# One store for the transposed logit rows, and W1's columns in blocks of 32, in a two-layer graph kernel

## The chip, the cores and the metric

One core of a Trainium2 chip. The metric is the device time of one execution in microseconds, median of the runs. The batch holds 128 graphs of 128 nodes with 512 features.

## The reference, cut to what matters

Each graph goes through a graph-attention layer and then a two-step hypergraph layer, each with a layer norm in front and a residual around it.

```python
# layer 0, per graph: h = relu(layernorm(x))
feats = einsum('bnf,hfu->bhnu', h, W)                   # 8 heads x 64
dense = e_self[..., :, None] + e_neigh[..., None, :]    # needs e_neigh of all nodes in every row
att   = softmax(leaky_relu(dense, 0.2) + NEG_BIG * (1 - A))
x     = x + relu(einsum('bhij,bhju->bhiu', att, feats) + b)
# layer 1: h = relu(layernorm(x)); H = (adj != 0)
r = relu(Dn * (H @ (Be * (H.T @ (h @ W1.T)))) + b1)     # 128 x 1024
h = layernorm(r) * gamma + beta
x = x + Dn * (H @ (Be * (H.T @ (h @ W2.T)))) + b2 + x
```

## The kernel before, in words

One graph is one turn; the instruction stream of each engine is written out by hand in a function `turn(t)`, and `turns` calls it for the first turns, for a loop unrolled by four, and for the last. A turn works on several graphs at once: it does attention's end for graph t+1, the projections of graph t+3, W1's product for graph t and W2's product for graph t-1. Products are made of three matmuls each (`three`, `high`, `low`), since every operand is split into a rounded half (`_hi`) and a remainder (`_lo`). In a turn TensorE does, in this order: W1's product into `p_w1a` and `p_w1b` (lines 866 and 869), the last product of graph t-2 into `p_tb` (898), the attention transposes (907), half of the projections (919), the attention product (927), W2's product (941 and 944), `p_w1b` from `h` and `G_rs` (957), the rest of the projections, and `p_G` (976).

Two things cross the partitions through DRAM, both on the queue of SyncE (SP), and both are touched by the change.

- **Logit rows.** `e_blk` holds 32 columns for each of the 128 nodes: the neighbour logits of the 8 heads and, for a later graph, the mean of its layer norm (9 rows wanted, `ROWS`). VectorE's transpose by blocks of 32 (line 651) gives `eT`, in which the 32 rows stand four times, once for each block of 32 nodes. Lines 275 and 276 store them with four DMAs of 9 partitions x 32 elements into `en_rows`, one semaphore (`s_en_out`) counts all four, line 277 waits for it, and line 278 reads `en_rows` back, broadcast to all 128 partitions, into `u`. GpSimd adds the mask to `u` (line 338) and then makes `xc` (347). VectorE takes the maximum (731) and, in order behind it, `shifts` (740), the attention's division and `x1` (747 to 757), the statistics of `x1` (760 to 778), `G_rs` (783) and `z` (797); ScalarE makes `h` (538), `z_hi` (547) and `hg_hi` (554). TensorE needs `h` and `G_rs` at line 957 and `hg_hi` at the start of the next turn.
- **r's transpose.** `r` is 128 x 1024. VectorE transposes it by blocks of 32 (line 722) into `rB`; line 289 stores it, line 290 waits, and lines 291 to 293 read it back with four DMAs. Each reads, for one quarter of a block row, runs of 32 elements (128 bytes): 32 partitions x 8 x 4 runs, 1,024 in a DMA. ScalarE rounds `rT` to `rT_hi` (561), VectorE takes the rest, `rT_lo` (658), and TensorE uses both a turn later (941, 944).

The four lines of the logit rows:

```python
for q in range(4):
    sp.dma_start(en_rows[:, 32 * q:32 * (q + 1)], eT[32 * q:32 * q + ROWS, :]).then_inc(s_en_out, 16)
sp.wait_ge(s_en_out, g.count(per=64))
sp.dma_start(u[:, g.slot(2), :, :]..., en_rows...broadcast_to([P, ROWS * N])).then_inc(s_en_bc, 16)
```

SP's order in a turn is: load `xT` of t+4, load `adj` of t+5, the logit rows, the store of the output of t-2, the store of `r_blocks` and its four reads. `x` is loaded by ScalarE's queue.

Of the kernel before, what the change touches and what calls it, by code (L numbers as in the profile page):

```python
# [4 lines left out]
F32 = mybir.dt.float32  # L5
F32R = mybir.dt.float32r
ALU = mybir.AluOpType
ACT = mybir.ActivationFunctionType
X = mybir.AxisListType.X

P = 128
# [38 lines left out]
def turns(eng, turn, total, before={}):  # L50


    loops = (total - AHEAD - 3) // UNROLL
    for t in range(-AHEAD, 2):
        if t in before:
            before[t]()
        turn(Graph(t))
    with eng.Fori(0, loops) as k:
        for u in range(2, UNROLL + 2):
            turn(Graph(u, k))  # L60
    for t in range(2 + loops * UNROLL, total + 2):
        turn(Graph(t))


def gnn_two_layers(nc, x, xT, adj2, W0T, W0U, b0, a_diag, W1T, b1, gammaT, betaT, W2T, b2, out):
    NG, N, D = x.shape
# [11 lines left out]
    ROWS = HEADS + 1  # L78

    ctx = ExitStack()  # L80
    with ctx:
        def sb(name, shape, dt=F32):
            return ctx.enter_context(nc.sbuf_tensor(name, shape, dt))

        def sem(name):
            return ctx.enter_context(nc.semaphore(name))
# [43 lines left out]
        eT = sb("eT", [P, 32])  # L130
# [10 lines left out]
        h = sb("h", [P, 2, D])  # L141
# [2 lines left out]
        r = raw[:, 2, 0:DH]  # L144
        rB = raw[:, 0, 0:DH]
        rT = raw[:, 0, DH:2 * DH]
        rT_hi, rT_lo = sb("rT_hi", [P, DH], F32R), sb("rT_lo", [P, DH], F32R)
        z = raw[:, 1, 3 * D:4 * D]
        z_hi, z_lo = sb("z_hi", [P, D], F32R), sb("z_lo", [P, D], F32R)
# [31 lines left out]
        s_e_blk, s_es_low, s_eT, s_en_out, s_en_bc, s_u = (sem("s_" + n) for n in ("e_blk", "es_low", "eT", "en_out", "en_bc", "u"))  # L181
# [7 lines left out]
        s_nm2a, s_nm2, s_sq2, s_ve2, s_rs2, s_rB, s_rB_out, s_rT, s_rT_hi, s_rT_lo = (sem("s_" + n) for n in ("nm2a", "nm2", "sq2", "ve2", "rs2", "rB", "rB_out", "rT", "rT_hi", "rT_lo"))  # L189
        s_w2, s_z, s_z_hi, s_z_lo, s_y, s_y_sb = (sem("s_" + n) for n in ("w2", "z", "z_hi", "z_lo", "y", "y_sb"))  # L190
        s_G_hi, s_G_lo = sem("s_G_hi"), sem("s_G_lo")

        en_rows = nc.dram_tensor("en_rows", [ROWS, N], F32, kind="Internal").ap()

        r_blocks = nc.dram_tensor("r_blocks", [P, DH], F32, kind="Internal").ap()

# [13 lines left out]
        def piece(n):  # L210
            return raw[:, n % 4, :].rearrange("p (c n) -> p c n", c=4)
# [12 lines left out]
        @block.sync  # L224
        def _(sp):
            def nth(g):
                return g.base if g.loop is None else g.loop * UNROLL + g.base

            def load_x(g):

                sp.dma_start(x_in[:, g.slot(4), :], x[bass.ds(nth(g), 1), :, :].rearrange("a p d -> p (a d)")).then_inc(s_in[g.slot(4)], 16)

            def load_adj(g):

                if g.has(4):
                    sp.wait_ge(s_inc, g.count(4))
                    sp.wait_ge(s_mask, g.count(4))
                    sp.wait_ge(s_row, g.count(4))
                sp.dma_start(adj_in[:, g.slot(4), :, :], adj2[bass.ds(nth(g), 1), :, :, :].rearrange("a p t n -> p (a t) n")).then_inc(s_in[g.slot(4)], 16)

            def load(g):
                load_x(g)
                load_adj(g)

            def load_xT(g):

                if g.has(2):
                    sp.wait_ge(s_xc, g.count(2))
                sp.dma_start(xT_in[:, g.slot(2), :, :],
                             xT[bass.ds(nth(g), 1), :, :, :].rearrange("a p c n -> p (a c) n")).then_inc(s_xT[g.slot(2)], 16)  # L250

            def load_last_piece():

                sp.wait_ge(k_hi, 1)
                sp.wait_ge(k_lo0, 1)
                sp.dma_start(piece(4), PIECES[4][0]).then_inc(s_raw[4], 16)

            def bc(v, n):
                return v.rearrange("(a n) -> a n", a=1).broadcast_to([P, n])

            load(Graph(0))
            load_xT(Graph(0))
            sp.dma_start(a_sb[:, :, :, :], a_diag).then_inc(s_vectors, 16)
            load(Graph(1))

            def turn(t):
                g = t.plus(4)
                if g.within(NG) and (g.loop is not None or g.base >= 2):
                    load_xT(g)
                if t.plus(5).within(NG) and (t.loop is not None or t.base >= -1):  # L270
                    load_adj(t.plus(5))
                if g.within(NG + 2):

                    sp.wait_ge(s_eT, g.count())
                    for q in range(4):
                        sp.dma_start(en_rows[:, 32 * q:32 * (q + 1)], eT[32 * q:32 * q + ROWS, :]).then_inc(s_en_out, 16)
                    sp.wait_ge(s_en_out, g.count(per=64))
                    sp.dma_start(u[:, g.slot(2), :, :].rearrange("p h n -> p (h n)"),
                                 en_rows.rearrange("(a h) n -> a (h n)", a=1).broadcast_to([P, ROWS * N])).then_inc(s_en_bc, 16)
                g = t.plus(-2)  # L280
                if g.within(NG):

                    sp.wait_ge(s_y_sb, g.count())
                    sp.dma_start(out[bass.ds(nth(g), 1), :, :].rearrange("a p d -> p (a d)"), y[:, g.slot(2), :]).then_inc(s_out[g.slot(2)], 16)
                g = t
                if g.within(NG):

                    sp.wait_ge(s_rB, g.count())
                    sp.dma_start(r_blocks[:, :], rB).then_inc(s_rB_out, 16)
                    sp.wait_ge(s_rB_out, g.count(per=16))  # L290
                    for c in range(4):
                        sp.dma_start(rT[32 * c:32 * (c + 1), :].rearrange("a (k q b) -> a k q b", q=4, b=32),
                                     r_blocks.rearrange("(q a) (k c b) -> c a k q b", q=4, c=4, b=32)[c]).then_inc(s_rT, 16)

            def setup_rest():
                load_xT(Graph(1))
                sp.dma_start(b0_bc[:, :], bc(b0.rearrange("h u -> (h u)"), D)).then_inc(s_small, 16)
                sp.dma_start(gamma_beta[:, 0, :], gammaT).then_inc(s_small, 16)
                sp.dma_start(gamma_beta[:, 1, :], betaT).then_inc(s_small, 16)
                load(Graph(2))  # L300
                load(Graph(3))
                sp.dma_start(b1_bc[:, :], bc(b1, DH)).then_inc(s_small, 16)
                sp.dma_start(b2_bc[:, :], bc(b2, D)).then_inc(s_small, 16)
                load_last_piece()

            turns(sp, turn, NG, {-3: setup_rest})
            for i in range(2):
                sp.wait_ge(s_out[i], 16 * (NG // 2))
# [96 lines left out]
        def _(act):  # L405
# [37 lines left out]
            def turn(t):  # L443
# [3 lines left out]
                g = t.plus(3)  # L447
# [6 lines left out]
                g = t  # L454
# [4 lines left out]
                g = t  # L459
# [5 lines left out]
                g = t.plus(2)  # L465
# [7 lines left out]
                g = t  # L473
# [3 lines left out]
                g = t.plus(1)  # L477
# [11 lines left out]
                g = t  # L489
# [13 lines left out]
                g = t.plus(-1)  # L503
# [5 lines left out]
                g = t  # L509
# [5 lines left out]
                g = t  # L515
# [8 lines left out]
                g = t.plus(5)  # L524
                if g.within(NG) and (g.loop is not None or g.base >= 4):

                    act.wait_ge(s_x1, g.count(4))
                    n = g.base if g.loop is None else g.loop * UNROLL + g.base
                    act.dma_start(x_in[:, g.slot(4), :], x[bass.ds(n, 1), :, :].rearrange("a p d -> p (a d)")).then_inc(s_in[g.slot(4)], 16)
                g = t.plus(1)  # L530
# [10 lines left out]
                g = t.plus(-1)  # L541
# [6 lines left out]
                g = t.plus(1)  # L548
# [6 lines left out]
                g = t  # L555
                if g.within(NG):

                    act.wait_ge(s_rT, g.count(per=64))
                    if g.has(1):
                        act.wait_ge(s_w2, g.count(1))  # L560
                    nc.scalar.activation(rT_hi[:, :], rT, ACT.Copy).then_inc(s_rT_hi, 1)  # L561
                g = t.plus(2)
                if g.within(NG):

# [11 lines left out]
            def setup_w2b():  # L576
                rounded(4)

            turns(act, turn, NG, {-2: setup_w1a, -1: setup_w1b, 0: setup_w2b})

        @block.vector
        def _(dve):
# [35 lines left out]
            def turn(t):  # L618
                g = t.plus(2)
# [34 lines left out]
                g = t.plus(-1)  # L654
                if g.within(NG):

                    dve.wait_ge(s_rT_hi, g.count())
                    nc.vector.tensor_tensor(rT_lo[:, :], rT, rT_hi[:, :], ALU.subtract).then_inc(s_rT_lo, 1)
                g = t
                if g.within(NG):  # L660

# [8 lines left out]
                g = t.plus(3)  # L670
# [5 lines left out]
                g = t.plus(2)  # L676
# [8 lines left out]
                g = t.plus(2)  # L685
# [13 lines left out]
                g = t  # L699
# [4 lines left out]
                g = t.plus(-2)  # L704
# [8 lines left out]
                g = t  # L713
# [13 lines left out]
                g = t.plus(2)  # L727
# [14 lines left out]
                g = t.plus(1)  # L742
# [18 lines left out]
                g = t.plus(2)  # L761
# [8 lines left out]
                if t.plus(1).within(NG):  # L770
                    g = t.plus(1)
# [18 lines left out]
                g = t.plus(-1)  # L790
# [8 lines left out]
                g = t.plus(5)  # L799
# [11 lines left out]
                if g.within(NG):  # L811
                    nc.vector.bn_aggr(mv0, st0[:, :]).then_inc(s_mv0, 1)

            turns(dve, turn, NG, {-3: setup_w0})

        @block.tensor
# [204 lines left out]
```

## Time and profile before

| | |
|---|---|
| median of 3 runs | 2489.99 us (2489.61 to 2491.07) |
| the profiled execution | 2479.36 us |
| its span, first to last instruction | 2477.6 us |
| TensorE busy | 2419.2 us, 98% of the span |
| VectorE, ScalarE, GpSimd busy | 1976.4, 1763.3, 1368.0 us |
| mean granted TensorE clock | 0.991 |
| DMA | 656,793 packets, 336.69 MB; 554,752 packets under 512 bytes |

The busy time of an engine is the sum of its instructions' time, in which overlapping matmuls count once; the ends of matmuls are modelled. An idle time stands in brackets behind an instruction in the timeline, with what ended it. SPq is SyncE's queue: a row of it is the issuing of a DMA, not its flight.

### The profile page before, as it was taken

What the parts mean: (1) busy time and instruction counts of PE and PEld (TensorE: products, weight loads), DVE (VectorE), ACT (ScalarE), POOL (GpSimd) and SP (SyncE); (2) the same over time, 40 slices, a digit from 0 to 9 for tenths busy, and PEclk for the clock granted to TensorE, in tenths of its full rate; (3) what the DMA queues carried; (4) which work ended last, traced back from release to release, by engine and by line L of the source; (5) the groups of instructions that cost most, each with busy time, mean ns of one, the idle gap of its engine ahead of it and who ended that gap; (6) DMA issues with size and microseconds to landing.
All of it is one profiled execution on the core that took longest, in us unless ns stands there. A gap on an engine that the chain in (4) does not pass through costs nothing.

```text
span 2477.6 us, 50428 instructions
## 1 busy us (share of the span) xinstructions
PE 2419.2 (98%) x14004; PEld 2101.6 (85%) x14004; DVE 1976.4 (80%) x4373; ACT 1763.3 (71%) x4489; POOL 1368.0 (55%) x1549
## 2 busy tenths in 40 slices
PE   5799999999999999999999999999999999999997
PEld 3688888888888888888888888888888888888886
DVE  3888888888888888888888888888888888888884
ACT  2677777777777777777777777777777777777774
POOL 2465555565565565565555555555555556556543
PEclk8899999999999999999999999999999999999999
DMA  5344454455445445445445445445454444445442
GB/s 206 95 139 138 136 140 137 134 140 140 134 139 141 134 139 141 134 138 142 132 138 143 131 139 143 125 145 139 128 142 137 134 138 138 137 137 138 138 113 72
DMA packets 656793, 336.69 MB, mean 136 GB/s; under 512 B 554752, under 2 KB 571136, under 8 KB 656768
## 3 DMA queue, kind: packets, MB, share of 16 engines
q1 hardware_dynamic: 636256, 298.64, 43.5%
q10 hardware_dynamic: 20512, 37.76, 4.3%
q8 instruction: 11, 0.18, 0.0%
q14 instruction: 14, 0.11, 0.0%
HBM read 235.03 MB, written 101.26 MB: 136 GB/s over the span
## 4 chain that ended last, share of the span: by engine, by line
PE 95%; DMA 2%; DVE 1%; issue 1%; ACT 1%; POOL 0%; SPq 0%; POOLq 0%; DVEq 0%; ACTq 0%
PE p_w1a L853 15%; PE p_w1a L858 14%; PE p_w1a L854 14%; PE p_att L927 9%; PE p_w1b L854 5%; PE p_w1b L858 5%; PE p_w1b L853 5%; PE p_w1b L957 5%; PE p_att L907 4%; PE p_fa L849 3%; PE p_fa L847 3%; PE p_fa L848 3%; PE p_fb L847 2%; PE p_fb L848 2%; PE p_fb L849 2%; PE p_tb L847 1%
## 5 line engine op out<-in xcount | busy, mean ns | idle before, releaser
L338 POOL TENSOR_TENSOR u<-u,mask 128x1024 f32<-128x1024 f32 x128 | 306.6, 2395 | 761.4 <-DMA u<-en_rows 761.4
L438 ACT ACTIVATE att<-u,shifts 128x128 f32<-128x128 f32 x1024 | 402.3, 393 | 133.0 <-DVE shifts L740 131.6
L853 PE MATMUL p_w1a<-W_hi,rT_hi 128*128 128x512 f32 x1024 | 416.8, 407 | 1.5 <-ACT rT_hi L561 1.5
L854 PE MATMUL p_w1a<-W_lo,rT_hi 128*128 128x512 f32 x1024 | 405.9, 396 | 0.0
L439 ACT ACTIVATE att_low<-u,shifts 128x128 f32<-128x128 f32 x1024 | 399.6, 390 | 0.0
L731 DVE TENSOR_REDUCE neg_max<-u 128x8 f32<-128x1024 f32 x128 | 156.1, 1220 | 149.9 <-POOL u L338 149.9
L858 PE MATMUL p_w1a<-W_hi,rT_lo 128*128 128x512 f32 x1024 | 259.5, 395 | 0.0
L392 POOL TENSOR_TENSOR z_lo<-raw,z_hi 128x512 fp32r<-128x512 f32 x128 | 165.7, 1294 | 154.9 <-ACT z_hi L547 154.9
L927 PE MATMUL p_att<-feats,attT 128*128 128x65 f32 x2048 | 243.1, 272 | 3.1 <-ACT attT L483 3.1
L927 PEld LDWEIGHTS p_att<-feats,attT 128*128 128x128 f32 x2048 | 239.5, 192 | 3.9 <-ACT attT L483 3.9
L547 ACT ACTIVATE z_hi<-raw 128x512 fp32r<-128x512 f32 x128 | 81.1, 634 | 221.6 <-DVE raw L797 221.6
L858 PEld LDWEIGHTS p_w1a<-W_hi,rT_lo 128*128 128x128 f32 x1024 | 192.4, 188 | 46.6
L853 PEld LDWEIGHTS p_w1a<-W_hi,rT_hi 128*128 128x128 f32 x1024 | 194.0, 189 | 42.5 <-ACT rT_hi L561 2.0
L854 PEld LDWEIGHTS p_w1a<-W_lo,rT_hi 128*128 128x128 f32 x1024 | 193.7, 189 | 40.6
L476 ACT ACTIVATE raw<-raw 128x512 f32<-128x512 f32 x128 | 80.8, 631 | 192.1 <-DVE raw L702 192.1
L853 PE MATMUL p_w1a<-W_hi,hg_hi 128*128 128x512 f32 x512 | 213.9, 418 | 2.2 <-ACT hg_hi L554 2.2
L853 PE MATMUL p_w1b<-W_hi,hg_hi 128*128 128x512 f32 x512 | 202.7, 396 | 0.0
L854 PE MATMUL p_w1b<-W_lo,hg_hi 128*128 128x512 f32 x512 | 202.3, 395 | 0.0
L854 PE MATMUL p_w1a<-W_lo,hg_hi 128*128 128x512 f32 x512 | 202.1, 395 | 0.0
L362 POOL TENSOR_TENSOR raw<-x,raw 128x512 f32<-128x512 f32 x128 | 166.1, 1298 | 26.9 <-DVE shifts L740 26.9
L347 POOL TENSOR_TENSOR xc<-xT_in,u 128x512 f32<-128x512 f32 x128 | 167.4, 1308 | 22.4 <-DMA u<-en_rows 22.4
L610 DVE TENSOR_TENSOR att<-att,att_low 128x512 f32<-128x512 f32 x256 | 174.3, 681 | 4.8 <-ACT att_low L439 4.8
(121 smaller groups left out, 6759.7 us busy)
## 6 DMA issues: line engine op xcount, KB each, us to landing
u<-en_rows SPq DMA_DIRECT2D x130, 576.0 KB, 3.6
r_blocks<-raw SPq DMA_DIRECT2D x128, 512.0 KB, 2.6
raw<-r_blocks SPq DMA_DIRECT2D x512, 128.0 KB, 3.2
xT_in<-in_xT SPq DMA_DIRECT2D x128, 256.0 KB, 3.9
out<-raw SPq DMA_DIRECT2D x128, 256.0 KB, 2.0
x_in<-in_x ACTq DMA_DIRECT2D x124, 256.0 KB, 3.6
adj_in<-in_adj SPq DMA_DIRECT2D x128, 128.0 KB, 2.5
en_rows<-eT SPq DMA_DIRECT2D x520, 1.1 KB
```

What stands on the lines that cost most here:

```text
L338: nc.gpsimd.tensor_tensor(u[:, g.slot(2), 0:HEADS, :], u[:, g.slot(2), 0:HEADS, :], mask[:, :].unsqueeze(1).broadcast_to([P, HEADS, N]), A ...
L347: nc.gpsimd.tensor_tensor(xc[:, :, :], xT_in[:, g.slot(2), :, :], u[:, g.slot(2), HEADS, :].unsqueeze(1).broadcast_to([P, DC, N]), ALU.sub ...
L362: nc.gpsimd.tensor_tensor(rest[s4], x1[:, s, :], rest[s4], ALU.add).then_inc(s_xh, 1)
L392: nc.gpsimd.tensor_tensor(z_lo[:, :], z[:, :], z_hi[:, :], ALU.subtract).then_inc(s_z_lo, 1)
L438: nc.scalar.activation(att[:, i, :], u[:, g.slot(2), i, :], ACT.Exp, bias=shifts[:, 0, i:i + 1])
L439: last = nc.scalar.activation(att_low[:, i, :], u[:, g.slot(2), i, :], ACT.Exp, bias=shifts[:, 1, i:i + 1], scale=SLOPE)
L610: nc.vector.tensor_tensor(att[:, heads, :], att[:, heads, :], att_low[:, heads, :], ALU.max).then_inc(s_att, 1)
L731: nc.vector.reduce_max(neg_max[:, :], u[:, g.slot(2), 0:HEADS, :], X, negate=True).then_inc(s_max, 1)
L853: mm(dst, hi, w_hi, start=first, stop=False)
L854: mm(dst, hi, w_lo, start=False, stop=False)
L858: return mm(dst, lo, w_hi, start=False, stop=final)
L927: last = mm(p_o[:, i // HH, i % HH, :], attT[:, i, :], feats[:, g.slot(2), i, :], start=True, stop=True)
```

## The change

The four stores of logit rows become one: all 128 partitions of `eT` are stored, 32 elements each, into an `en_rows` of 32 rows in place of 9, of which the broadcast reads the first 9 as before. The wait behind it counts 16 in place of 64. The columns of W1 and the entries of b1 are laid out on the host in another order (`by_blocks`), with which `r`'s columns that one of the four reads fetches stand next to each other: each read takes runs of 256 elements (1 KB), 32 partitions x 4 runs, 128 in a DMA. The data in `rT` then stand in another order within a partition, and lines 561 and 658 read them through a view of four dimensions (`rT_chunks`) in runs of 32 elements; what they write is laid out as before. The rest of the kernel is as it was.

```diff
--- before.py
+++ after.py
@@ -144,6 +144,7 @@
         r = raw[:, 2, 0:DH]
         rB = raw[:, 0, 0:DH]
         rT = raw[:, 0, DH:2 * DH]
+        rT_chunks = rT.rearrange("p (q k a) -> p k q a", q=4, a=32)
         rT_hi, rT_lo = sb("rT_hi", [P, DH], F32R), sb("rT_lo", [P, DH], F32R)
         z = raw[:, 1, 3 * D:4 * D]
         z_hi, z_lo = sb("z_hi", [P, D], F32R), sb("z_lo", [P, D], F32R)
@@ -190,7 +191,7 @@
         s_w2, s_z, s_z_hi, s_z_lo, s_y, s_y_sb = (sem("s_" + n) for n in ("w2", "z", "z_hi", "z_lo", "y", "y_sb"))
         s_G_hi, s_G_lo = sem("s_G_hi"), sem("s_G_lo")
 
-        en_rows = nc.dram_tensor("en_rows", [ROWS, N], F32, kind="Internal").ap()
+        en_rows = nc.dram_tensor("en_rows", [32, N], F32, kind="Internal").ap()
 
         r_blocks = nc.dram_tensor("r_blocks", [P, DH], F32, kind="Internal").ap()
 
@@ -272,11 +273,10 @@
                 if g.within(NG + 2):
 
                     sp.wait_ge(s_eT, g.count())
-                    for q in range(4):
-                        sp.dma_start(en_rows[:, 32 * q:32 * (q + 1)], eT[32 * q:32 * q + ROWS, :]).then_inc(s_en_out, 16)
-                    sp.wait_ge(s_en_out, g.count(per=64))
+                    sp.dma_start(en_rows.rearrange("h (q a) -> q h a", a=32), eT[:, :]).then_inc(s_en_out, 16)
+                    sp.wait_ge(s_en_out, g.count(per=16))
                     sp.dma_start(u[:, g.slot(2), :, :].rearrange("p h n -> p (h n)"),
-                                 en_rows.rearrange("(a h) n -> a (h n)", a=1).broadcast_to([P, ROWS * N])).then_inc(s_en_bc, 16)
+                                 en_rows[0:ROWS, :].rearrange("(a h) n -> a (h n)", a=1).broadcast_to([P, ROWS * N])).then_inc(s_en_bc, 16)
                 g = t.plus(-2)
                 if g.within(NG):
 
@@ -289,8 +289,8 @@
                     sp.dma_start(r_blocks[:, :], rB).then_inc(s_rB_out, 16)
                     sp.wait_ge(s_rB_out, g.count(per=16))
                     for c in range(4):
-                        sp.dma_start(rT[32 * c:32 * (c + 1), :].rearrange("a (k q b) -> a k q b", q=4, b=32),
-                                     r_blocks.rearrange("(q a) (k c b) -> c a k q b", q=4, c=4, b=32)[c]).then_inc(s_rT, 16)
+                        sp.dma_start(rT[32 * c:32 * (c + 1), :].rearrange("a (q n) -> a q n", q=4),
+                                     r_blocks.rearrange("(q a) (c n) -> c a q n", q=4, c=4)[c]).then_inc(s_rT, 16)
 
             def setup_rest():
                 load_xT(Graph(1))
@@ -558,7 +558,7 @@
                     act.wait_ge(s_rT, g.count(per=64))
                     if g.has(1):
                         act.wait_ge(s_w2, g.count(1))
-                    nc.scalar.activation(rT_hi[:, :], rT, ACT.Copy).then_inc(s_rT_hi, 1)
+                    nc.scalar.activation(rT_hi[:, :].rearrange("p (k q a) -> p k q a", q=4, a=32), rT_chunks, ACT.Copy).then_inc(s_rT_hi, 1)
                 g = t.plus(2)
                 if g.within(NG):
 
@@ -655,7 +655,8 @@
                 if g.within(NG):
 
                     dve.wait_ge(s_rT_hi, g.count())
-                    nc.vector.tensor_tensor(rT_lo[:, :], rT, rT_hi[:, :], ALU.subtract).then_inc(s_rT_lo, 1)
+                    nc.vector.tensor_tensor(rT_lo[:, :].rearrange("p (k q a) -> p k q a", q=4, a=32), rT_chunks,
+                                            rT_hi[:, :].rearrange("p (k q a) -> p k q a", q=4, a=32), ALU.subtract).then_inc(s_rT_lo, 1)
                 g = t
                 if g.within(NG):
 
@@ -997,6 +998,10 @@
     for k, a in enumerate((L0_gnn_a_neigh, L0_gnn_a_self)):
         for p in range(2):
             a_diag[p, :, :, k, p] = np.asarray(a)[p::2, :].T
+    def by_blocks(a):
+
+        return a.reshape(a.shape[:-1] + (-1, 4, 32)).swapaxes(-3, -2).reshape(a.shape)
+
     laid = {
         "x": x,
         "xT": np.asarray(x).transpose(0, 2, 1).reshape(len(x), -1, P, np.asarray(x).shape[1]).transpose(0, 2, 1, 3),
@@ -1004,7 +1009,7 @@
         "W0T": np.asarray(L0_gnn_W).transpose(1, 0, 2).reshape(f, -1),
         "W0U": np.asarray(L0_gnn_W).transpose(0, 2, 1).reshape(-1, f),
         "b0": L0_gnn_b, "a_diag": a_diag.reshape(2 * units, heads // 2, 2, 2),
-        "W1T": np.asarray(L1_gnn_W1).T, "b1": L1_gnn_b1,
+        "W1T": by_blocks(np.asarray(L1_gnn_W1).T), "b1": by_blocks(np.asarray(L1_gnn_b1)),
         "gammaT": np.asarray(L1_gnn_gamma).reshape(-1, P).T, "betaT": np.asarray(L1_gnn_beta).reshape(-1, P).T,
         "W2T": np.asarray(L1_gnn_W2).T, "b2": L1_gnn_b2,
     }
```

## Rows read from the trace of the kernel before

**Rows 1.** Page, part 1: busy time of each engine.

```profile
PE 2419.2 (98%) x14004; PEld 2101.6 (85%) x14004; DVE 1976.4 (80%) x4373; ACT 1763.3 (71%) x4489; POOL 1368.0 (55%) x1549
```

**Rows 2.** Busy time of each engine in one stretch of 200 us.

```profile
1000.00:1200.00 200.00, 199.99 (x1164) 174.20 (x1164) 164.35 (x368) 147.44 (x379) 114.52 (x131) 1.00 0.49 137
```

**Rows 3.** Waits of TensorE: total, times, longest, in us.

```profile
PE p_w1b L957 <- ACT h L538: 14.1, 2, 10.6
```

**Rows 4.** Timeline of TensorE, line 976 alone: start, duration; six turns of 128.

```profile
114.32 0.39 PE L976 MATMUL p_tb<-beT,inc 128*128 128x129 f32 x2
...
1679.35 0.39 PE L976 MATMUL p_tb<-beT,inc 128*128 128x129 f32 x2
...
1698.35 0.39 PE L976 MATMUL p_tb<-beT,inc 128*128 128x129 f32 x2
...
2034.65 0.39 PE L976 MATMUL p_tb<-beT,inc 128*128 128x129 f32 x2
...
2201.99 0.39 PE L976 MATMUL p_tb<-beT,inc 128*128 128x129 f32 x2
...
2407.06 0.39 PE L976 MATMUL p_tb<-beT,inc 128*128 128x129 f32 x2
```

**Rows 5.** Timeline of the turn from 1679.35, SP, GpSimd, VectorE and TensorE.

```profile
1681.53 1.37 SPq L276 DMA_DIRECT2D en_rows<-eT  x4
1683.80 0.34 SPq L278 DMA_DIRECT2D u<-en_rows  x1
...
1687.67 2.37 POOL L338 TENSOR_TENSOR u<-u,mask 128x1024 f32<-128x1024 f32 x1 [6.43 <-DMA u<-en_rows]
...
1695.72 0.31 DVE L783 TENSOR_SCALAR G_rs<-G,rs 128x128 f32<-128x128 f32 x1 [0.71 <-POOL rs L373]
...
1696.28 1.15 PE L957 MATMUL p_w1b<-G_rs,h 128*128 128x128 f32 x8
```

**Rows 6.** Timeline of the turn from 2164.80, the same two engines.

```profile
2171.94 2.41 POOL L338 TENSOR_TENSOR u<-u,mask 128x1024 f32<-128x1024 f32 x1 [5.59 <-DMA u<-en_rows]
...
2181.42 1.05 PE L957 MATMUL p_w1b<-G_rs,h 128*128 128x128 f32 x8
```

**Rows 7.** Page, part 6: DMA issues, KB each, median us to landing.

```profile
r_blocks<-raw SPq DMA_DIRECT2D x128, 512.0 KB, 2.6
...
out<-raw SPq DMA_DIRECT2D x128, 256.0 KB, 2.0
...
adj_in<-in_adj SPq DMA_DIRECT2D x128, 128.0 KB, 2.5
```

**Rows 8.** Issues of r_blocks on SP: duration ns min/median/max.

```profile
L292 SPq DMA_DIRECT2D raw<-r_blocks x512: 568/683/1488, 88.2 to 2458.5; - x171
L289 SPq DMA_DIRECT2D r_blocks<-raw x128: 319/327/385, 85.6 to 2453.8; - x128
```

**Rows 9.** Chain that ended last, first 60 us, two of four stores.

```profile
22.40 7.52 DMA en_rows<-eT
...
35.41 1.19 DMA en_rows<-eT
```

**Rows 10.** Timeline of the last turn, SP, ScalarE and TensorE.

```profile
2456.47 2.75 SPq L292 DMA_DIRECT2D raw<-r_blocks  x4
...
2461.53 1.06 ACT L561 ACTIVATE rT_hi<-raw 128x1024 fp32r<-128x1024 f32 x1 [2.79 <-DMA raw<-r_blocks]
...
2460.71 0.40 PE L849 MATMUL p_tb<-z_hi,G_lo 128*128 128x512 f32 x1
2462.64 0.80 PE L853 MATMUL p_w1a<-W_hi,rT_hi 128*128 128x512 f32 x1 [1.54 <-ACT rT_hi L561]
```

**Rows 11.** VectorE by line: busy, mean ns of one, idle before it.

```profile
L731 DVE TENSOR_REDUCE neg_max<-u 128x8 f32<-128x1024 f32 x128 | 156.1, 1220 | 149.9 <-POOL u L338 149.9
...
L749 DVE TENSOR_TENSOR p_ta<-p_att,rden 128x512 f32<-128x512 f32 x128 | 89.6, 700 | 4.4
...
L757 DVE SCALAR_TENSOR_TENSOR x<-p_ta,x_in 128x512 f32<-128x512 f32 x128 | 88.5, 691 | 4.4
```

## The prediction, made before the change was run

> **What bounds the kernel now.** The page's first part gives TensorE 98% of the time, VectorE 80% [rows 1], and a stretch of 200 us in the middle has TensorE busy all through [rows 2]. The list of its waits agrees: the large ones lie in the first 100 us and the last 65, as the one of 10.6 us for `h` [rows 3]. By these three views only the two ends could be won. But the ends of matmuls are modelled, so a late start can hide in a busy time. The fourth view therefore is the start of one fixed instruction in each turn (line 976) [rows 4]. The nine turns from 2034.65 to 2201.99 take 167.34 us, 18.593 each: TensorE's own pace. The 123 turns from 114.32 to 2407.06 take 2292.74 us; at 18.593 they would take 2286.97. So **5.8 us** are lost in the middle, in small pieces, where no wait is listed. The turn from 1679.35 to 1698.35 alone takes 19.00, which is 0.41 too long.
>
> What do the long turns have in common? In that one GpSimd's mask addition, released by the landing of `u<-en_rows`, starts 8.32 us after the turn's line 976; in a turn at the pace of 18.59 it starts 7.14 after it [rows 5, 6]. From there the chain runs through VectorE's maximum, the attention's end and `G_rs`; `G_rs` ends at 1696.03 and line 957, which needs it, starts 0.25 later, 16.93 into the turn, where the other turn has it at 16.62. So TensorE is held 0.31 us there, and the rest of the 0.41 follows at `hg_hi`, made behind it. The slack of this chain ends where the mask addition starts some 8.0 us into the turn (8.32 less 0.31). It is also nearly a loop: VectorE's `eT` stands in its order behind `hg_lo` of the turn before, so a late `u` makes the next `eT` late. I went through all 124 turns in this way: the turns over 18.63 are those with the latest `u`, or the ones just behind them. The store of the logit rows lies on this chain.
>
> **The change, part by part.**
>
> *One store for four.* From the first issue to the broadcast behind the wait there are 2.27 us (1681.53 to 1683.80), of which four issues take 1.37, 0.34 each [rows 5]. The last starts at about 1682.56, so a store of 9 packets has landed 1.2 us after its issue; the chain gives 1.19 for one in the first turns [rows 9]. Three issues go, 1.03 us. What comes in their place is a store of 128 packets of 128 bytes, which the trace does not have. From below it is the 1.2 of 9 packets. From above it is the output's store, also one packet for each of 128 partitions, but 256 KB: 2.0 us; `r_blocks`, 512 KB, takes 2.6 [rows 7], so the size costs 0.6 per 256 KB, and at 16 KB that line comes down to 1.4. Small writes may be dearer than their bytes, so I take 1.6, the middle of 1.2 and 2.0. The broadcast then starts 2.27 - 1.6 = 0.67 us earlier in each turn; the bounds are 0.27 and 1.07.
>
> In the middle this buys no TensorE time as such; it moves `u` from 8.32 to 7.65 in the latest turn, below 8.0. It would do so with 0.32 already. Term: **-5.8 us**; at the bound of 0.27 the latest turns keep a little, say -5. What is late next is TensorE itself, so nothing more is to be had: 18.593 is the floor.
>
> In the first turns there are four such stores on the chain that sets the start. Two of them land under the load of the weights and `x`, 7.52 us after the last issue in the worse case [rows 9]; their landing is not set by when they are issued, and I take nothing, with 1 us either way. The other two are as in the middle, on the chain before TensorE's continuous work begins: 2 x 0.67 = **-1.3 us** (0.5 to 2.1).
>
> *The reads of r's transpose.* Each has 1,024 packets and takes 0.683 us to issue; an issue with 128 packets, `r_blocks`' own store, takes 0.327 [rows 8]. Four reads: 1.4 us less of SP's time in each turn, in which only `xT` and `adj` stand behind them, loaded turns ahead. `rT_hi` is ready long before its use in the next turn, so in the middle the gain is worth nothing. In the last turn nothing covers it. There the reads are issued from 2456.47 on, in 2.75 us, and ScalarE starts `rT_hi` at 2461.53 [rows 10]. At 0.36 from issue to issue the last one starts at 2457.55; `adj_in` is 128 KB in runs of 1 KB as well and lands in 2.5 us [rows 7], so `rT_hi` starts at 2460.05. Term: **-1.5 us**. TensorE, which now starts at 2462.64, would start at 2461.1; its product in front has its last start at 2460.71 [rows 10], so not much more than 1.6 can come. If the landing stays as it is, 1.05. The first seven matmuls behind this wait are 0.43 us apart where 0.23 is usual, at the lower level of the clock; if the shorter wait spares that, up to 1.3 us more, which I leave to the range.
>
> *The view in runs of 32* in lines 561 and 658: the nearest row is line 749, which works in runs of 64 with a gap, 700 ns, beside line 757, contiguous, 691 ns [rows 11]. Nothing, or 0.02 us; VectorE's wait for `u`, 149.9 / 128 = 1.17 us a turn [rows 11], covers it, and still 0.5 of it is there when `u` comes 0.67 sooner. The host's order of W1 and b1 costs nothing: the same loads, the same columns to TensorE.
>
> **Sum:** 5.8 + 1.3 + 1.5 = 8.6 us. The profiled execution's 2479.36 becomes 2470.8; the median is 10.6 us longer than that execution, and with the same difference it becomes **2481.4 us**, -0.35%. About 0.2% (5 us) is what a measurement of this kernel can tell from no change.
>
> **Rivals.**
>
> *Only the ends (0.22).* The 5.8 us stay, because something else than `u` makes the long turns, or because the executions without a profile, 10.6 us longer, lose their time elsewhere. For it: the waits' list names no such wait, and ScalarE waited for `rT` now and then. Against it: the order of the start times in the two turns. Then 1.3 + 1.5 = 2.8: 2487.2.
>
> *The wide store is slow (0.13), the one that ends slower.* Its packets could go one behind another on few DMA engines. Price: 32 in a row. At the pace of the reads, 1,024 packets on 16 engines in 0.683 us, that is 10.7 ns each, 0.34 us in all, so a store of 1.54 us, and the forecast stands. At 75 ns, what the 8 packets of an engine cost more at 4 KB than at 2 KB (0.6 us / 8) [rows 7], it is 2.4 us, a store of 3.6, 1.33 later than now. Even the good turn with its 0.86 of slack (7.14 to 8.0) would then stall by 0.47, x 124 = 58 us: 2548. It decides from 33 ns a packet on, where the store is as long as now (1.2 + 32 x 0.033).
>
> The Trainium skill has the rule for this (DMA: Bandwidth & Descriptors, "Why a DMA increments its semaphore by 16 and not by 1"): a DMA uses the largest number of engines up to 16 that divides the slowest dimension of both sides. By that rule this store, whose DRAM side has 4 as its slowest dimension, would run on 4 engines, 32 packets on each; no row here shows it. The same page's table (Specifications) has writes under 512 bytes done as read-modify-write, which speaks for the dearer price. [...]
>
> *The views of 32 cost (0.04).* VectorE and ScalarE stand in the chain; only once line 658 takes 1.17 + 0.67 us longer than its wait allows, each 0.1 us more costs 12 us. At double the time of 561 and 658, 1.2 us more, it is still covered, so it needs 2.5 times or more: then 2490 and up. Line 749 speaks against it.
>
> *More than the trace shows (0.07).* If half of the 10.6 us by which plain executions are longer are stalls of the same sort, they go as well: 2476.
>
> **The numbers.** Forecast 0.54, only the ends 0.22, wide store 0.13, views 0.04, more 0.07. Faster by over 0.2%: 0.54 + 0.07, 0.61. Within: 0.22. Slower: 0.13 + 0.04 = 0.17. The range from 2475 to 2488.5 holds the forecast with its bounds (5 + 0.5 + 1.05 = 6.5, to 5.8 + 2.1 + 1.6 + 1.3 and the 1 us of the loaded stores, 11.8), the ends alone and the larger gain.
>
> **What would show it.** Line 276 issues once a turn, in about 0.33 us, and line 277's broadcast starts 1.4 to 1.9 us after it; the mask addition never starts later than 8.0 after line 976; turns at 18.59 throughout, 123 of them in 2287. Packets fall from 656,793 to some 210,000. The four reads take 1.4 us on SP, not 2.75. If the broadcast starts 2.3 us or more behind the store, the store's term is wrong; if it is early and long turns remain, the reading of the middle is; if line 561 or 658 exceeds 1.06 or 1.22 us, the views' price is.

## The result and the profile after

The changed kernel takes **2472.76 us** (median of 4 runs, 2470.57 to 2477.86) against 2490.53 for the kernel before in the same comparison: a ratio of 0.9932, 95% interval 0.9918 to 0.9946, 17.8 us less. The forecast was 8.6 us less, with a range down to 2475. The direction was right; the size was half of what came, and the time lies below the range.

The page after, of its parts 1, 3 and 6 the lines that matter (part 6: KB each, median us from issue to landing), then the issues of the logit rows' store and of the four reads (ns, min/median/max):

```profile
PE 2417.0 (98%) x14004; PEld 2101.0 (85%) x14004; DVE 1986.0 (80%) x4373; ACT 1766.1 (71%) x4489; POOL 1369.9 (55%) x1549
...
DMA packets 205840, 338.19 MB, mean 137 GB/s; under 512 B 38264, under 2 KB 120184, under 8 KB 205816
...
u<-en_rows SPq DMA_DIRECT2D x130, 576.0 KB, 3.8
raw<-r_blocks SPq DMA_DIRECT2D x512, 128.0 KB, 2.8
```

```profile
L276 SPq DMA_DIRECT2D en_rows<-eT x130: 520/547/672, 9.6 to 2409.1; - x130
```

```profile
L292 SPq DMA_DIRECT2D raw<-r_blocks x512: 302/425/436, 90.5 to 2456.9; - x171
```

Busy times and shares say nothing new beside [rows 1]. What answers to [rows 4] does. The start of the instruction that opens a turn (now line 977), for the first and last turn of the middle and for the same nine turns, with the turn that answers to [rows 5] among them:

```profile
120.72 0.39 PE L977 MATMUL p_tb<-beT,inc 128*128 128x129 f32 x2
...
1682.63 0.39 PE L977 MATMUL p_tb<-beT,inc 128*128 128x129 f32 x2
...
2035.91 0.39 PE L977 MATMUL p_tb<-beT,inc 128*128 128x129 f32 x2
...
2203.24 0.39 PE L977 MATMUL p_tb<-beT,inc 128*128 128x129 f32 x2
...
2407.77 0.39 PE L977 MATMUL p_tb<-beT,inc 128*128 128x129 f32 x2
```

Nine turns are 167.33 us, as before. The 123 turns are 2287.05 us, where 123 x 18.593 is 2286.94: the 5.8 us of small stalls are down to 0.1. The turn that starts at 1682.63, seen on SP, GpSimd and TensorE:

```profile
1684.48 0.56 SPq L276 DMA_DIRECT2D en_rows<-eT  x1
1686.46 0.33 SPq L278 DMA_DIRECT2D u<-en_rows  x1
...
1690.13 2.39 POOL L338 TENSOR_TENSOR u<-u,mask 128x1024 f32<-128x1024 f32 x1 [5.94 <-DMA u<-en_rows]
...
1699.25 1.05 PE L958 MATMUL p_w1b<-G_rs,h 128*128 128x128 f32 x8
```

From issue to broadcast 1.98 us instead of 2.27, the mask addition 7.50 into the turn instead of 8.32, and the product from `G_rs` at 16.62, the place it has in an undisturbed turn.

This execution, the slowest of its four (2477.86 us), gives most of it back at the start: its middle begins at 120.72, not at 114.32. Of these 6.4 us, 4.1 arise in the last turn of the start, which takes 23.0 us instead of 18.9, and two things make most of them. The first is told by two rows, VectorE and GpSimd:

```profile
104.55 2.17 DVE L697 TENSOR_SCALAR cnt<-G 128x2 f32<-128x2 f32 x1
```

```profile
104.31 2.39 POOL L338 TENSOR_TENSOR u<-u,mask 128x1024 f32<-128x1024 f32 x1 [5.82 <-DMA u<-en_rows]
```

An operation on two elements a partition takes 2.17 us instead of 0.17 and ends at 106.72, with the mask addition that began 0.24 before it (106.70). The Trainium skill has this (SBUF — State Buffer, "Who interferes with whom"): VectorE in a two-port mode, which `tensor_scalar` can enter, and GpSimd share a pair of ports, and whichever starts first holds it for its whole instruction, while the other stands still. The two rows agree; no row names the mode. It happened in one of the fourteen traces; in the middle line 697 is over about 1 us before `u` lands.

The second follows from it. TensorE waits for `attT`, two microseconds longer than in the kernel before, and behind that wait the granted clock is 0.50, the lower of its two levels, from 110.4 to 113.7:

```profile
109.29 2.74 PE L928 MATMUL p_att<-feats,attT 128*128 128x65 f32 x16 [2.15 <-ACT attT L483]
```

Its matmuls then start up to 0.43 us apart instead of 0.23, which adds some 1.6 us.

### The profile page after: what moved, and what is told of

The parts are those of the page before. It is cut to its first block, busy times and chain, and to the rows that moved or that the text cites. A ratio compares the mean times of both kernels' runs of the same rounds, so it can differ in the third digit from the quotient of the medians.

```text
span 2476.1 us, 50038 instructions
## 1 busy us (share of the span) xinstructions
PE 2417.0 (98%) x14004; PEld 2101.0 (85%) x14004; DVE 1986.0 (80%) x4373; ACT 1766.1 (71%) x4489; POOL 1369.9 (55%) x1549
## 4 chain that ended last, share of the span: by engine, by line
PE 96%; DMA 1%; DVE 1%; issue 1%; ACT 1%; SPq 0%; POOL 0%; POOLq 0%; ACTq 0%; DVEq 0%
PE p_w1a L854 15%; PE p_w1a L859 14%; PE p_w1a L855 14%; PE p_att L928 9%; PE p_w1b L855 5%; PE p_w1b L859 5%; PE p_w1b L854 5%; PE p_w1b L958 5%; PE p_att L908 4%; PE p_fa L850 3%; PE p_fa L848 3%; PE p_fa L849 3%; PE p_fb L848 2%; PE p_fb L849 2%; PE p_fb L850 2%; PE p_tb L848 1%
```

## The experiments

The four comparisons below ran on four chips, with medians of 2481.3 to 2483.4 us for the kernel before; the first had 2490.5. So times are set against the kernel before of the same comparison. Traces are split in four: the start (until the middle's first turn), the middle (what the next 123 turns take over 123 x 18.593), the last but one turn, the rest.

### One part at a time

The kernel before and the changed one again, and each half of the change alone. Store alone:

```diff
-for q in range(4):
-    sp.dma_start(en_rows[:, 32 * q:32 * (q + 1)], eT[32 * q:32 * q + ROWS, :]).then_inc(s_en_out, 16)
-sp.wait_ge(s_en_out, g.count(per=64))
+sp.dma_start(en_rows.rearrange("h (q a) -> q h a", a=32), eT[:, :]).then_inc(s_en_out, 16)
+sp.wait_ge(s_en_out, g.count(per=16))
```

Reads alone: the other lines of the change.

> The kernel before, unchanged, in the same rounds as the three others. Theory 1 (long turns come from a late u, and the timed executions have more of them than the profiled one of the prediction): where the time is near 2490, the turns between line 976 at about 120 us and 2425 us hold 12 to 16 us more than 124 x 18.593 us, with the mask addition starting later than 8.0 us into the long ones. Rival (the ends): the middle holds about 6 us too much as in the first trace, and the other 10 us lie in the first 120 us or the last 50.

> The changed kernel, unchanged. Both theories: 2470 to 2478 us. Theory 1: no turn over 18.63 us in the middle. The first 120 us differ from run to run by several us in place (turns 0 to 2).

> Only the store is changed: one DMA of 128 packets for four; the reads of r's transpose stay at 128 bytes. Theory 1: nearly all of the gain, 12 to 17 us under the kernel before, no long turns. Rival 1 (the small packets of the reads hold up the landing of other DMAs, and the reads' change is what removes the long turns): under 4 us of gain, long turns stay.

> Only the reads are changed: runs of 1 KB; the store stays in four DMAs. Theory 1: 1.5 to 3 us of gain, from the last turn, long turns stay as in the kernel before. Rival 1: 12 us or more of gain, and the broadcast of u lands sooner after its issue.

| kernel | median us | start | middle over | last but one turn | rest |
|---|---|---|---|---|---|
| before | 2483.53 (2482.38 to 2485.92) | 116.4 | 9.5 | 18.6 | 52.7 |
| changed | 2471.10 (2470.57 to 2472.36) | 113.3 | 0.0 | 17.0 | 51.4 |
| store alone | 2472.49 (2471.51 to 2473.91) | 114.7 | 0.2 | 17.0 | 52.3 |
| reads alone | 2482.30 (2480.04 to 2484.53) | 116.1 | 9.8 | 18.6 | 51.3 |

The columns behind the median are of the one traced execution of each. The ratios, to all executions of the kernel before in this comparison (median 2482.97): store alone 0.9956 (0.9942 to 0.9969), changed 0.9952 (0.9938 to 0.9965), reads alone 0.9997 (0.9988 to 1.0006). The store is 11.0 of the 12.4 us. The reads alone are worth 1.2, a difference that the interval doesn't tell from none, but the last column has it in both pairs: 1.4 and 0.9 us. The packets that fell from 656,793 to 198,041 with the reads did nothing for the middle, and `u` lands no sooner after its issue (3.73 us, 3.71 in the kernel before), so rival 1 falls. How the middle reads in the trace of the kernel before here, first and last turn:

```profile
116.37 0.39 PE L976 MATMUL p_tb<-beT,inc 128*128 128x129 f32 x2
...
2412.82 0.39 PE L976 MATMUL p_tb<-beT,inc 128*128 128x129 f32 x2
```

2296.45 us for 123 turns, where [rows 4] had 2292.74. The same kernel thus loses 5.8 us in one execution and 9.5 in another. The last turn, SP and ScalarE, before:

```profile
2462.22 2.78 SPq L292 DMA_DIRECT2D raw<-r_blocks  x4
...
2467.24 1.06 ACT L561 ACTIVATE rT_hi<-raw 128x1024 fp32r<-128x1024 f32 x1 [2.74 <-DMA raw<-r_blocks]
```

and changed:

```profile
2448.15 1.74 SPq L292 DMA_DIRECT2D raw<-r_blocks  x4
...
2452.41 1.06 ACT L561 ACTIVATE rT_hi<-raw 128x1024 fp32r<-128x1024 f32 x1 [1.99 <-DMA raw<-r_blocks]
```

From the first issue to `rT_hi` 4.26 us instead of 5.02.

### Is it when u lands?

Three kernels put DMAs back into the changed one. Their packets are small and go to a scratch tensor.

```diff
+for i in range(1):          # 2 in the second kernel
+    sp.dma_start(en_scratch[i], eT[0:ROWS, :]).then_inc(s_en_out, 16)
 sp.dma_start(en_rows.rearrange("h (q a) -> q h a", a=32), eT[:, :]).then_inc(s_en_out, 16)
-sp.wait_ge(s_en_out, g.count(per=16))
+sp.wait_ge(s_en_out, g.count(per=32))   # 48
```

In the third the extra DMA is issued behind line 278's broadcast, from `ident`, and counted by a semaphore of its own.

> The changed kernel with one more DMA of 9 packets issued in front of the store and counted by the same wait, 0.31 us of SP's time, so that issue to broadcast takes about 2.27 us as before the change. Theory 1 (what counts is when u lands): the middle loses its 9 us again, 2479 to 2486 us. Rival 2 (it is the number or kind of the packets, or how many DMAs the wait counts, whatever the time): stays at 2471 to 2473.

> The same with two such DMAs in front, 0.62 us. Theory 1: u is 0.3 us later than in the kernel before and the loss grows faster than in proportion, since turns that had slack now have none: 2495 to 2525 us, with the turns over 18.63 us in the majority. Rival 2: 2471 to 2474.

> The changed kernel with one more DMA of 9 packets, issued behind the broadcast of u instead of in front of the store. The same work for SP and the DMA engines, and u is not later. Theory 1: 2470 to 2473 us, no long turns. Rival 3 (SP's queue as a whole is what is tight): 2475 us or more.

One issue in front: 2484.83 us (2479.42 to 2487.14), ratio to the kernel before 1.0013 (1.0003 to 1.0023). All of the gain is gone with 0.31 us of SP's time, though the store is still the one wide DMA and the wait counts two. Two issues: **2533.26 us**, 8 us above what I had allowed, ratio 1.0208 (1.0191 to 1.0225). Behind the broadcast: 2471.38, ratio 0.9959 (0.9945 to 0.9973), where the changed kernel had 0.9952. The same DMA in the same turn costs nothing or 13 us, by the side of `u` on which it stands, so rivals 2 and 3 fall. The middle with two in front, where the turn's first instruction stands in line 981:

```profile
116.39 0.39 PE L981 MATMUL p_tb<-beT,inc 128*128 128x129 f32 x2
...
2462.99 0.38 PE L981 MATMUL p_tb<-beT,inc 128*128 128x129 f32 x2
```

2346.60 us, 59.7 over TensorE's pace, 0.49 a turn.

### What the 128 packets cost

```diff
-sp.dma_start(en_rows.rearrange("h (q a) -> q h a", a=32), eT[:, :]).then_inc(s_en_out, 16)
+sp.dma_start(en_rows.rearrange("(h b) (q a) -> (h b q) a", b=1, a=32), eT[:, :]).then_inc(s_en_out, 16)
```

This kernel leaves out the placing of the logits by head in `en_rows`; every engine has the same work.

> The changed kernel with the DRAM side of the store in the order of the partitions, one piece of 16 KB; the logits land in the wrong places, so the attention is not the reference's, all else is. Tests what the 128 packets cost: if they run on 4 engines one behind another in the changed kernel, issue to broadcast falls from 1.96 to about 1.6 us here and the issue from 0.55 to 0.33 us. If a store of 128 packets costs that anyhow: 1.9 to 2.0 us. The time stays at 2470 to 2472 either way, since the middle is at TensorE's pace.

```profile
1007.79 0.33 SPq L276 DMA_DIRECT2D en_rows<-eT  x1
1009.22 0.33 SPq L278 DMA_DIRECT2D u<-en_rows  x1
```

1.43 us from issue to broadcast and 0.33 for the issue, lower than I expected even here, against 1.97 and 0.56 in the changed kernel. The packets are as many and as long; only the order on the DRAM side differs. That is the rule weighed in the prediction (the Trainium skill, DMA: Bandwidth & Descriptors, "Why a DMA increments its semaphore by 16 and not by 1"), by which, beside the 128 partitions of `eT`, a DRAM side with 4 as its slowest dimension gets 4 engines and one with 128 gets 16. No row names the engines, but the packets tell. The 2 us from the issue on, in 40 slices of 0.05 us, first in the changed kernel, then with the flat store:

```profile
GB/s 0 0 0 0 0 0 0 0 0 0 0 0 0 0 0 0 0 0 0 0 0 0 0 3 36 54 54 56 54 51 21 0 0 0 0 0 0 0 0 0
DMA packets 132, 0.02 MB, mean 8 GB/s; under 512 B 132, under 2 KB 132, under 8 KB 132
```

```profile
GB/s 0 0 0 0 0 0 0 0 0 0 0 0 0 0 0 0 31 102 113 64 18 0 0 0 0 0 0 0 0 0 0 0 0 0 0 0 0 0 0 0
DMA packets 144, 0.02 MB, mean 8 GB/s; under 512 B 144, under 2 KB 144, under 8 KB 144
```

Beside the 128 packets of data there are 4 packets of 4 bytes in the one and 16 in the other, and 9 for each of the four old stores of 9 partitions: the numbers of engines that the rule gives. The data packets fill 0.37 us against 0.22; in the changed kernel four of them start every 9.4 ns, the pace of one packet after another on four engines. But of the 0.54 us between the two kernels this is only 0.15. The first packet starts 1.18 us after the issue against 0.83, which is 0.35, and the broadcast follows the last packet by 0.42 against 0.38. Why the first packet is later is open; the issue itself takes 0.22 longer, and the two layouts also differ in how the pieces lie in DRAM.

The median is 2471.08 (2470.23 to 2479.05), so 0.5 us more of slack for `u` buy no time.

The same with two issues in front lies between the changed kernel and the one before:

> The flat store of the earlier run (the logits land in the wrong places, so the attention is not the reference's) with two DMAs of 9 packets issued in front. Issue to broadcast is then about 2.1 to 2.2 us, 2.4 from eT on, between the changed kernel (2.20 from eT) and the kernel before (2.50). Theory 1 (the time hangs on when u lands, steeply past a point): the middle loses 1 to 5 us, 2473 to 2480 us. Rival 2 (number of DMAs that the wait counts): three as in the kernel with 2533 us, so far above 2490.

2475.75 us (2474.43 to 2477.36), ratio 0.9972 (0.9960 to 0.9983), with three DMAs counted by the wait, as in the kernel of 2533 us. So it is not the number of DMAs counted that costs. And the kernel before once more:

> The kernel before once more, for its trace on another chip or at another time. Theory 1: 2478 to 2491 us, and whatever it is above the last trace lies in the middle, with the mask addition later on average; 1.6 us in the last but one turn are lost again to the lower level of the clock.

2483.70 (2481.55 to 2485.60), middle 10.5 over, start 115.0. Its last but one turn takes 17.0 us, not 18.6, against what I had expected.

Put together, the mean start of the mask addition in a turn against what the middle loses (my own table, from the start times of 120 turns in each trace; the second column runs from the start of the transpose that writes `eT`; the traces are of several chips):

| trace | from eT to broadcast | mask addition starts | latest | middle over |
|---|---|---|---|---|
| flat store | 1.67 | 6.66 | 7.68 | 0.0 |
| issue behind | 2.19 | 7.24 | 7.78 | 0.0 |
| changed (this comparison) | 2.20 | 7.25 | 7.80 | 0.0 |
| changed (first trace) | 2.20 | 7.34 | 7.86 | 0.1 |
| store alone | 2.22 | 7.28 | 7.99 | 0.2 |
| flat store, two issues in front | 2.41 | 7.58 | 8.37 | 3.4 |
| before (first trace) | 2.50 | 7.68 | 8.33 | 5.8 |
| before (this comparison) | 2.50 | 7.78 | 8.57 | 9.5 |
| reads alone | 2.51 | 7.80 | 8.48 | 9.8 |
| before, again | 2.50 | 7.82 | 8.55 | 10.5 |
| one issue in front | 2.55 | 7.81 | 8.57 | 10.9 |
| two issues in front | 2.94 | 8.42 | 9.12 | 59.7 |

One curve holds for all: flat up to 7.3, then steep, some 35 us for a microsecond near 7.7 and, by the one point beyond, about 80 from 7.8 on. It also shows the chain closing on itself. From the kernel before (9.5) to the changed one the store gives 0.30 us, yet the mask addition comes 0.53 earlier: the other 0.24 is `eT`, which starts 1.34 into the turn instead of 1.58, since the turn before it was no longer late. The three traces of one unchanged kernel differ in the landing of `u` by 0.06 us (3.67, 3.70 and 3.73 from the broadcast's issue) and in the middle by 4.7 us.

### What makes a turn late: a miss

> The kernel before with the loop over the turns unrolled by eight in place of four. In the traces the long turns are nearly all those that open a pass of the loop, in which VectorE's eT comes 0.35 us later than in the others, before the first instruction that reads p_fa. Theory 1 with this trigger: half as many such turns, so the middle loses about half as much, 3 to 5 us less than the kernel before, and the long turns stand eight apart. Rival 4 (the long turns come from the DMA traffic, whatever the loop): no change, long turns as many as before.

> The changed kernel, unrolled by eight. Theory 1: within 1.5 us of the changed kernel, 2470 to 2473, since every turn is at TensorE's pace already.

```diff
-UNROLL = 4
+UNROLL = 8
```

2564.49 us (2562.09 to 2567.22) and 2540.69 (2540.27 to 2541.95): both far slower, against all that was expected. The changed kernel, unrolled by eight: its waits for "issue" (total, times, longest, in us) and its instruction queues on the page:

```profile
DVE e_blk L630 <- issue: 70.2, 15, 5.3
ACT att L438 <- issue: 36.3, 14, 2.7
...
PE p_w1a L854 <- issue: 25.3, 14, 2.0
```

```profile
q8 instruction: 140, 2.29, 0.4%
q14 instruction: 187, 1.53, 0.2%
```

Where the first of these queues moves 0.18 MB in the changed kernel, it moves 2.29 MB with the body twice as long, and VectorE stands 4.7 us at each of the 15 passes. By these rows the longer body fetches its instructions anew in each pass. Of the 69.5 us that its middle loses, 67.9 lie in the turns that open a pass; with the kernel before it is 77.7 of 90.2. The test of the trigger was spoilt by this. What stays of it comes from the traces alone: with the body of four, `eT` starts 1.62 us into the turn that opens a pass and 1.22 to 1.29 into the others (changed kernel), and of the 5.8 us of the first trace 4.1 lie in those turns, of the 9.5 of the second 5.6. They are not nearly all of the long turns, as I had it before the run: 19 of 28 over 18.63 us in the first trace, 21 of 45 in the second. That a branch costs VectorE 0.4 us there, and that this is what starts the long turns, fits but was not shown by an experiment.

## Why the prediction was right and wrong

- **What bounds the middle:** right. The stalls that no list of waits names were there, `u`'s landing sets them, and they go with the store. The point where they begin, put at 8.0 us for a single turn, fits too: the traces whose latest turn stays under 8.0 lose 0.2 us at most.
- **The size of that term:** this is the step that failed. The prediction took 5.8 us, from the one execution whose trace it had, as what every execution loses in the middle, and set the median, 10.6 us longer than that execution, apart as a difference that stays. The kernel before loses 9.5 and 10.5 us in the middle in two other traces, and all of it goes with the store. So 3.7 and 4.7 us more of the same are shown, where the 10.6 had been taken for something else. That was the rival "more than the trace shows", held at 0.07, and its price of half, 5.3 us, gave 2476, which is short as well. That the loss is steep in the lateness was in reach: [rows 5, 6] show a loop and a threshold, and a loss read at the edge of a threshold should have had a wide range.
- **The store:** 0.67 us earlier was forecast, 0.30 measured (from `eT` to the broadcast, 2.50 to 2.20), near the lower bound of 0.27. The rival that the wide store is slow had the four engines right. Its lower price, 10.7 ns a packet, is near the 9.4 of the trace, but by luck: it was worked out from the time that SP takes to issue the reads, not from their flight. It gave a store of 1.54 us and the forecast took 1.6, where 1.97 came, since neither had the later first packet (1.18 us after the issue, 0.77 in the kernel before). Yet 0.30 was enough, where the prediction asked for 0.32: the chain that closes on itself gave the rest.
- **The start:** -1.3 forecast; -3.0 between two traces of one comparison, but the start scatters from 114.3 to 116.4 us in the three traces of before and from 113.3 to 120.7 in the two of after. No term of this size can be read off it. The collision of VectorE and GpSimd in the last turn of the start, with the lower clock behind it, was not foreseen.
- **The end:** -1.5 forecast, 0.8 us sooner to `rT_hi` in the rows, 1.2 us (reads alone) and 1.4 (changed against store alone) in the medians. The issue with 128 packets takes 0.43, not 0.36. The lower level of the clock was not spared: in the changed kernel's last turn the matmuls behind `rT_hi` again start 0.43 apart, at a granted clock of 0.50.
- **The views of 32** cost nothing: lines 561 and 658 take 1053 and 1215 ns, 1055 and 1215 before.
- **The 17.8 us** of the first comparison against 12.4 of the second lie mostly in the kernel before, 2490.5 there and 2483.5 here; the changed one is at 2472.8 and 2471.1. By the curve a mean 0.1 us later than in the traces at hand would make up the difference, but no execution of the kernel before at 2490 us was traced, so where its 7 us more lie is argued, not shown.

## What to carry to other kernels

A busy time whose ends are modelled hides stalls: measure the distance between two starts of the same instruction, in every turn, and compare the shortest with the mean. Where a chain closes on itself just under the bound engine's period, a few tenths of a microsecond decide over tens, and one execution doesn't tell how much is lost; give the chain slack first, and stop once the turns are at the bound's pace. When several DMAs become one, look at the slowest dimension of both sides: here a layout with 4 there ran on four engines and gave back 0.54 us against one with 128.

## What the runs showed that was not expected

- Unrolling by eight in place of four costs some 70 us in the changed kernel and 80 in the one before, nearly all in the turns that open a pass of the loop.
- In the last but one turn TensorE waits 1.11 us for `attT` in either kernel, and then in two of three traces of the kernel before (and in that of the reads alone) eight matmuls start 0.43 us apart instead of 0.23, 1.6 us in all, at a granted clock of 0.50; in the third, and in those of the changed kernel, the clock stays at 1.00. The two cases, kernel before, same line:

```profile
2421.49 2.05 PE L927 MATMUL p_att<-feats,attT 128*128 128x65 f32 x16 [1.11 <-ACT attT L483]
2423.30 0.78 PE L853 MATMUL p_w1a<-W_hi,rT_hi 128*128 128x512 f32 x1
```

```profile
2421.12 2.00 PE L927 MATMUL p_att<-feats,attT 128*128 128x65 f32 x16 [1.11 <-ACT attT L483]
2422.93 0.48 PE L853 MATMUL p_w1a<-W_hi,rT_hi 128*128 128x512 f32 x1
```

  The same wait behind the same work goes either way, so which one comes isn't set by anything these rows show.
